# Query projections of head groups 2 to 8 by one level of Strassen's algorithm

## The chip, the cores and the metric

The kernel runs on one core of one Trainium2 chip. The metric is the device time of one execution in microseconds (us): before the change the median of 3 runs is 1006.12 us (1002.88 to 1007.81).

## The reference, cut to what matters

The program is one decoder layer in float32 on 8 blocks of 128 tokens with 512 channels: a Mamba2 mixer, a gated MLP, a cross attention with 32 query heads in 8 groups (each group has one key and value head), and a small gated LoRA layer, with norms between. The change touches the cross attention alone:

```python
for g in range(8):                              # head groups
    K = rms(ctx @ Wk[g].T) * k_norm_w           # 1024 x 128
    V = ctx @ Wv[g].T                           # 1024 x 128
    for h in range(4):                          # heads of the group
        Q = rms(x @ Wq[g, h].T) * q_norm_w      # x is 1024 x 512, Wq[g, h] is 128 x 512
        for b in range(8):                      # blocks of 128 tokens
            P = softmax(Q[b] @ K[b].T / sqrt(128) + mask)
            out[b] += (P @ V[b]) @ Wo[:, g, h].T
```

For a group, all of Q is one product: the weights (512 outputs by 512 channels) times the activations (512 channels by 1024 tokens).

## The kernel before, in words

Every engine has its own in-order instruction queue, written out by hand; engines meet through semaphores (`wait_ge`). A float32 operand is split into a rounded part and a remainder (`_hi`, `_lo`), and each product is three matmuls (`mm3`, L374 to L378): ScalarE writes `_hi`, GpSimd or VectorE subtracts it to give `_lo`.

The attention is a loop over groups g of eight slots jj, one for each block of 128 tokens. Slot jj does the attention of block jj, and beside it a piece of the projections that later slots need: n = jj // 4 is a half of the tokens, j = jj % 4. In each slot TensorE's queue (`slot` in the tensor block) holds, in this order:

- the query product of one head over 512 tokens (`q_step`, 12 matmuls of 512 columns, in banks 0 and 1), and the key and value products of one token block (`kv_step`, 12 matmuls of 256 columns, bank 2). Slots 3 and 7 have no `kv_step`; they begin with `kt_step` (L641), which transposes the normed keys in bank 0 or 1. Slots 0 and 4 have two `kv_step`
- `s_step` (L654), the scores of the next block in bank 3
- `pt_step` (L664), the transposes of this block's probabilities
- `d_step`, 12 matmuls: the output projection of the block before
- in slots 2 and 6 `qs_step` (L635), which folds the sums of squares of four heads in bank 7
- `pv_step`, 3 matmuls: probabilities times values.

The other queues follow it. VectorE in a slot: sum of squares of one head (`q_part`, L1864 and L1866), in slots 2 and 6 `k_var`, `softmax_max` (L1901, L1905), `pt_rest`, `v_rest`, in slots 2 and 6 `k_norm` (L1855), `add_out` (L1923), `softmax_rec` (L1910), in slots 2 and 6 `q_var` (L1877, reads bank 7), `ot_rest`. ScalarE: `q_evac` (L1129 squares a head, L1132 copies it), `kv_evac`, `pt_evac`, `softmax_exp` (L1161), rounding of weights (`wq_hi` L1106, `wkv_hi` L1097, `wo_hi` L1115), `ot_evac`. GpSimd: powers for the norms (`k_rsqrt`, `q_rsqrt`), `p_scale` (L1509: scales the probabilities of the next block), and the `_lo` parts of weights (L1327): four pieces of 512 columns of query weights, four of output weights in slot 0, two of key and value weights in slot 2. SyncE loads the weights of the next group when the buffers `raw_a` and `raw_b` come free.

`kt_step` in slot 3 belongs to the keys whose norm was made in slot 2; it waits only for that norm and for the bank:

```python
def kt_step(g, n):
    pe.wait_ge(kn_done, 2 * g + n + 1)
    wait_bank(g, 5 * n + 4)
```

The query heads of group g are spread: the four of tokens 512 to 1023 in slots 7 (of group g - 1), 0, 1 and 2, the four of tokens 0 to 511 in slots 3 to 6 of group g - 1. The last group therefore still has one head in each of slots 0, 1 and 2. The loop is `Fori(0, 7)` over groups, with slot 0 of group 0 before it and slots 1 to 7 of the last group behind it.

Of the kernel before, what the change touches and what calls it, by code (L numbers as in the profile page):

```python
# [29 lines left out]
def build_program(nc, x, ctx_t, mask, consts, fold_in, chan, rows, w_dt, w_in, w_out, w_gu, w_dn,  # L30
# [9 lines left out]
    with ctx:  # L40
# [11 lines left out]
        act_hi = sb(ctx, "act_hi", [P, KT, B * L], f32r)  # L52
        act_lo = sb(ctx, "act_lo", [P, KT, B * L], f32r)
        res = sb(ctx, "res", [P, B, DM])
        w_hi = sb(ctx, "w_hi", [P, 5120], f32r)
        w_lo = sb(ctx, "w_lo", [P, 5120], f32r)
        raw_a = sb(ctx, "raw_a", [P, 2048])
        raw_b = sb(ctx, "raw_b", [P, 2048])
        cst = sb(ctx, "cst", [P, 3 * P])
        ident, tri, strict = cst[:, 0:P], cst[:, P:2 * P], cst[:, 2 * P:3 * P]  # L60
        chan_sb = sb(ctx, "chan_sb", [P, NCONV * DCONV + NCONV + 2])
        qk_w = sb(ctx, "qk_w", [P, 1])
        pow_m = sb(ctx, "pow_m", [P, 16])
        xn = sb(ctx, "xn", [P, 2, DM])
# [9 lines left out]
        with ExitStack() as m:  # L74
            row_sb = sb(m, "row_sb", [P, 2 * DM + 3 * NH])
# [30 lines left out]
        with ExitStack() as m:  # L106
# [21 lines left out]
            ra_sb = sb(m, "ra_sb", [P, KT, NE + NE * RANK])  # L128
            bl_sb = sb(m, "bl_sb", [NE * RANK, DM])
            cmp_m = sb(m, "cmp_m", [P, 2, NE, NE])  # L130
            lg = sb(m, "lg", [P, B, NE])
            dif = sb(m, "dif", [P, B, NE, NE])
            beat = sb(m, "beat", [P, B, NE, 2, NE])
# [5 lines left out]
            midt = sb(m, "midt", [NE * RANK, B, P])  # L139
# [3 lines left out]
            with ExitStack() as early:  # L143
                q2 = sb(early, "q2", [P, 2, NTOK])
                q2t = sb(early, "q2t", [P, NTOK])
            x2t = sb(m, "x2t", [P, 2, KT, P])
            mid = sb(m, "mid", [P, B, NE, RANK])
# [64 lines left out]
        d_mm, d_add = sem("d_mm"), sem("d_add")  # L212

# [3 lines left out]
        dl_cp, dl_pool, a_sum, a_mean, a_ssq = (sem("dl_cp"), sem("dl_pool"), sem("a_sum"), sem("a_mean"),  # L217
                                                sem("a_ssq"))
# [11 lines left out]
        WQ_SLOT = {1: (0, 1), 3: (2,), 4: (3,)}  # L230
# [26 lines left out]

        def mamba_raw(p):

            return raw_b[:, (p - 4) * 512:(p - 3) * 512] if 4 <= p < 8 else raw_a[:, p % 8 * 512:(p % 8 + 1) * 512]  # L260
# [3 lines left out]
        def _(sp_eng):  # L264
# [18 lines left out]
            sp_eng.dma_start(cst[:, P:], consts[:, P:]).then_inc(ld_small[6], 16)  # L283
# [61 lines left out]
            sp_eng.dma_start(mask_sb[:, :], mask).then_inc(ld_small[4], 16)  # L345
            sp_eng.dma_start(ra_sb[:, :, :], w_ra).then_inc(ld_lora[0], 16)
            sp_eng.dma_start(bl_sb[:, :], w_b).then_inc(ld_lora[1], 16)

            def next_group(g):


                sp_eng.wait_ge(wq_l, 4 * g + 4)
                sp_eng.dma_start(raw_a[:, :], w_q[bass.ds(g + 1, 1)].rearrange("a p n -> (a p) n"))\
                    .then_inc(ld_q, 16)
                sp_eng.wait_ge(wo_l, 4 * g + 4)
                sp_eng.dma_start(raw_b[:, 0:1024], w_kv[bass.ds(g + 1, 1)].rearrange("a p n -> (a p) n"))\
                    .then_inc(ld_kv, 16)
                sp_eng.wait_ge(wkv_l, 2 * g + 4)
                sp_eng.dma_start(raw_b[:, :], w_o[bass.ds(g + 1, 1)].rearrange("a p n -> (a p) n"))\
                    .then_inc(ld_o, 16)  # L360

            with sp_eng.Fori(0, GROUPS - 1) as g:
                next_group(g)
# [7 lines left out]
        def _(pe):  # L371
# [232 lines left out]
            def q_step(g, n, h):  # L604

                pe.wait_ge(wq_l, 4 * g + h + 1)
                r = 5 * n + h
                wait_bank(g, r)
                tok = slice(n * NTOK, (n + 1) * NTOK)
                for k in range(KT):  # L610
                    c0 = WQ_COL[h] + k * P
                    t = mm3(bank[r % 2][:, :], w_hi[:, c0:c0 + P], w_lo[:, c0:c0 + P],
                            act_hi[:, k, tok], act_lo[:, k, tok], k == 0, k == KT - 1)
                t.then_inc(q_mm, 1)

            def wait_bank(g, r):


                pr = (r - 2) % 10
                gg = g if r >= 2 else g - 1  # L620
                if isinstance(gg, int) and gg < 0:
                    return
                n, hh = pr // 5, pr % 5
                if hh < 4:
                    pe.wait_ge(q_ev, 8 * gg + 4 * n + hh + 1)
                else:
                    pe.wait_ge(kt_ev, 2 * gg + n + 1)

            def qs_step(g, n):
# [3 lines left out]
                if not (isinstance(g, int) and u == 0):  # L633
                    pe.wait_ge(qv_done, u)
                mm(bank[7][:, 0:GH * 16], fold[:, :], qpart[:, n, :], start=True, stop=True).then_inc(qs_mm, 1)  # L635

            def kt_step(g, n):
                pe.wait_ge(kn_done, 2 * g + n + 1)
                wait_bank(g, 5 * n + 4)
                for j in range(HALF):  # L640
                    t = nc.tensor.transpose(bank[(5 * n + 4) % 2][:, j * P:(j + 1) * P], kraw[:, j, :], ident)  # L641
# [48 lines left out]
            def slot(g, jj, lead=True, before=True):  # L690

                n, j = jj // HALF, jj % HALF
                pg, pn = (g, 1) if n == 0 else (g + 1, 0)
                if j == 0:
                    kv_step(pg, pn, 0)
                if j < 3:
                    q_step(pg, pn, j + 1)
                    kv_step(pg, pn, j + 1)
                else:
                    kt_step(pg, pn)  # L700
                    if lead:
# [1476 lines left out]
```

## Time and profile before

| | us |
|---|---|
| three runs | 1002.88, 1006.12, 1007.81 (median 1006.12) |
| the profiled execution, its own time | 1007.58 |
| its span in the profile | 1005.8 |
| TensorE busy in the span | 966.1 (96%) |
| VectorE, ScalarE, GpSimd busy | 573.8, 494.2, 404.0 |
| mean granted TensorE clock | 0.986 of full |

The profile page gives busy times by engine and by line; the timeline gives each instruction with its start and duration, and in brackets how long its engine sat idle before it and who released it. The duration of a matmul in it is longer than its share of the engine, because matmuls overlap: what one costs is the distance from one start to the next. A windows row is the busy time of each engine in a stretch, with the granted clock.

### The profile page before, as it was taken

To read this page: it belongs to the slowest core of one execution; us is meant where nothing else is said; L and a number is where in the kernel's file an instruction comes from. 1 tells how busy PE (TensorE), PEld (TensorE's weight loads), DVE (VectorE), ACT (ScalarE), POOL (GpSimd) and SP (SyncE) were. 2 spreads that over 40 slices of the span, in tenths; PEclk is the share of its full clock that TensorE was granted. 3 is DMA by queue.
4 is the path that set the end of the run, shared out by engine and by line. 5 is a ranking of instruction groups with operands and counts; after the bars stand their busy time and mean duration, and the time that the engine had idled before them with its cause. 6 is when DMAs were issued, how large, how long until landed. Compare 5 with 4: busy or idle time off the path is not lost.

```text
span 1005.8 us, 15353 instructions
## 1 busy us (share of the span) xinstructions
PE 966.1 (96%) x5010; PEld 804.8 (80%) x5010; DVE 573.8 (57%) x1340; ACT 494.2 (49%) x1368; POOL 404.0 (40%) x341
## 2 busy tenths in 40 slices
PE   5999799999999999899999999999999999999895
PEld 3866488878888888788888888888888888888782
DVE  3665554422321357566666666666566666666777
ACT  4655342422231246555654654654655555555554
POOL 4334634744443453342442442532622623514322
PEclk9999999999999999899999999999999999999997
DMA  6200013310111111011010020020020020100002
GB/s 218 82 3 31 12 46 125 105 63 0 63 63 63 44 62 56 22 43 43 22 54 29 21 83 0 21 83 0 21 83 0 27 78 0 63 0 0 1 1 85
DMA packets 12977, 45.60 MB, mean 45 GB/s; under 512 B 1617, under 2 KB 2257, under 8 KB 9873
## 3 DMA queue, kind: packets, MB, share of 16 engines
q1 hardware_dynamic: 12944, 45.20, 12.9%
q8 instruction: 17, 0.28, 0.1%
q14 instruction: 16, 0.12, 0.0%
HBM read 43.10 MB, written 2.10 MB: 45 GB/s over the span
## 4 chain that ended last, share of the span: by engine, by line
PE 86%; DVE 5%; POOL 3%; ACT 2%; issue 2%; DMA 1%; SPq 0%; POOLq 0%; DVEq 0%; ACTq 0%
PE bank L376 25%; PE bank L378 24%; PE bank L377 24%; PE bank L654 6%; PE bank L664 3%; PE bank L387 1%; POOL res L1438 1%; DVE cbuf L1638 1%; POOL rstd L1333 1%; PE bank L641 1%; DVE bst L1775 1%; POOL h_lo L1327 1%; DMA res<-in_x 1%; PE bank L455 1%; PE bank L744 0%
## 5 line engine op out<-in xcount | busy, mean ns | idle before, releaser
L376 PE MATMUL bank<-act_hi,w_hi 128*128 128x512 f32 x560 | 225.0, 402 | 2.0 <-DVE act_lo L1585 1.6
L378 PE MATMUL bank<-act_hi,w_lo 128*128 128x512 f32 x560 | 220.0, 393 | 0.0
L377 PE MATMUL bank<-act_lo,w_hi 128*128 128x512 f32 x560 | 220.0, 393 | 0.0
L1509 POOL TENSOR_TENSOR pb<-pb,prec 128x512 f32<-128x512 f32 x64 | 66.6, 1040 | 311.6 <-DVE prec L1910 311.6
L1161 ACT ACTIVATE pb<-pb,nmax 128x128 f32<-128x128 f32 x256 | 99.8, 391 | 79.1 <-DVE nmax L1905 79.1
L376 PEld LDWEIGHTS bank<-act_hi,w_hi 128*128 128x128 f32 x560 | 106.1, 189 | 25.6 <-issue 4.3
L378 PEld LDWEIGHTS bank<-act_hi,w_lo 128*128 128x128 f32 x560 | 106.1, 189 | 22.9
L377 PEld LDWEIGHTS bank<-act_lo,w_hi 128*128 128x128 f32 x560 | 106.2, 190 | 22.7 <-issue 1.4
L376 PE MATMUL bank<-w_hi,ot_hi 128*128 128x512 f32 x256 | 105.0, 410 | 0.8 <-DVE ot_lo L1585 0.8
L378 PE MATMUL bank<-w_hi,ot_lo 128*128 128x512 f32 x256 | 100.9, 394 | 0.0
L377 PE MATMUL bank<-w_lo,ot_hi 128*128 128x512 f32 x256 | 100.3, 392 | 0.0
L1327 POOL TENSOR_TENSOR w_lo<-raw_b,w_hi 128x512 fp32r<-128x512 f32 x70 | 89.2, 1298 | 10.4 <-ACT w_hi L845 10.4
L1129 ACT ACTIVATE q<-bank 128x512 f32<-128x512 f32 x64 | 38.2, 597 | 106.9 <-PE bank L378 106.9
L1327 POOL TENSOR_TENSOR w_lo<-raw_a,w_hi 128x512 fp32r<-128x512 f32 x66 | 85.0, 1306 | 4.2 <-ACT w_hi L845 2.2
L1327 POOL TENSOR_TENSOR h_lo<-hb,h_hi 128x512 fp32r<-128x512 f32 x28 | 37.4, 1336 | 120.5 <-ACT h_hi L1052 120.5
L1809 DVE TENSOR_TENSOR hb<-sg,bank 128x512 f32<-128x512 f32 x28 | 19.2, 687 | 115.9 <-ACT sg L1044 115.9
L1864 DVE STREAM_TRANSPOSE q2t<-q 128x512 f32<-128x512 f32 x64 | 45.3, 708 | 68.6 <-ACT q L1129 68.4
L1044 ACT ACTIVATE sg<-bank 128x512 f32<-128x512 f32 x28 | 16.7, 598 | 130.0 <-PE bank L378 130.0
L1901 DVE SCALAR_TENSOR_TENSOR pb<-bank,qr,mask_sb 128x128 f32<-128x128 f32 x256 | 71.9, 344 | 12.4 <-PE bank L654 11.1
L376 PE MATMUL bank<-w_hi,ctx_hi 128*128 128x256 f32 x256 | 72.3, 282 | 2.0 <-DVE kraw L1800 2.0
L1585 DVE TENSOR_TENSOR pt_lo<-bank,pt_hi 128x512 fp32r<-128x512 f32 x64 | 43.7, 683 | 51.1 <-ACT pt_hi L1169 51.1
L378 PE MATMUL bank<-w_hi,ctx_lo 128*128 128x256 f32 x256 | 72.0, 281 | 0.0
(190 smaller groups left out, 2066.4 us busy)
## 6 DMA issues: line engine op xcount, KB each, us to landing
raw_a<-in_w_q SPq DMA_DIRECT2D x8, 1024.0 KB, 4.8
raw_b<-in_w_o SPq DMA_DIRECT2D x8, 1024.0 KB, 4.8
raw_a<-in_w_gu SPq DMA_DIRECT2D x7, 1024.0 KB, 5.3
raw_b<-in_w_kv SPq DMA_DIRECT2D x8, 512.0 KB, 3.3
raw_b<-in_w_dn SPq DMA_DIRECT2D x7, 512.0 KB, 3.3
res<-in_x SPq DMA_DIRECT2D x8, 256.0 KB, 6.1
raw_b<-in_ctx_t SPq DMA_DIRECT2D x8, 256.0 KB, 3.2
xre<-in_x SPq DMA_DIRECT2D x2, 1024.0 KB, 7.0
```

Source lines behind the costliest of these rows:

```text
L376: mm(o, l_hi, r_hi, start=first, stop=False)
L377: mm(o, l_hi, r_lo, start=False, stop=False)
L378: return mm(o, l_lo, r_hi, start=False, stop=last)
L654: t = mm(bank[3][:, h * L:(h + 1) * L], q_t[:, n, h, tok], k_t[:, n, tok], start=True, stop=True)
L664: t = nc.tensor.transpose(bank[4][:, h * L:(h + 1) * L], pb[:, jj % 2, h, :], ident)
L1129: A(q2[:, h % 2, :], bank[(5 * n + h) % 2][:, :], ACT.Square).then_inc(qsq_done, 1)
L1161: t = A(pb[:, jj % 2, h, :], pb[:, jj % 2, h, :], ACT.Exp, bias=nmax[:, jj % 2, h:h + 1], accum_out=psum_[:, jj % 2, h:h + 1])
L1327: TT(dst, src, f32(hi), ALU.subtract).then_inc(done, 1)
L1509: TT(pb[:, jj % 2, :, :], pb[:, jj % 2, :, :], prec[:, jj % 2, :].unsqueeze(2).to_broadcast([P, GH, L]), ALU.mult).then_inc(p_norm, 1)
L1585: TT(dst, src, f32(hi), ALU.subtract).then_inc(done, 1)
L1864: V.transpose(q2t[:, :], q2[:, h % 2, :]).then_inc(qtr_done, 1)
L1901: t = STT(pb[:, jj % 2, h, :], bank[3][:, h * L:(h + 1) * L], qr[:, 4 * n + h, j:j + 1], mask_sb[:, :], ALU.mult, ALU.add)
```

## The change

Of the product weights times activations the weights are cut in four blocks (two by two heads, two by two halves of the channels: A11, A12, A21, A22 with 256 x 256 numbers each) and the activations in four (B11, B12, B21, B22: half of the channels by half of the tokens). Before, each head and token half took four channel steps: eight block products. Now, for groups 2 to 8, seven block products P1 to P7 of sums of blocks give the same four results (Strassen's algorithm in Winograd's form). One product is 2 (heads) x 2 (channel steps) x 3 = 12 matmuls of 512 columns. Group 1 (g = 0) is computed as before, its last three heads together in slot 0.

- The sums of activation blocks T1 to T4 are made once, in group 0: 20 operations of 512 columns on GpSimd (`combine_t3` and `combine_t1`, 12 of them, in slot 0; `combine_t2`, 6, in slot 1; `combine_t4`, 2, in slot 3), each waiting for the one before it, all ahead of `p_scale` of their slot. ScalarE rounds them, VectorE makes the remainders (`t_round`, `t_rest`).
- The sums of weight blocks are made per group, 4 operations on GpSimd (`combine_s`, `combine_s1`, `combine_s4`), and each of the seven operands is rounded and split on its own: 7 pieces on ScalarE and GpSimd for 4 (`wp_hi`, `wp_rest`).
- The sums of products are made by VectorE (`q_add`, 12 operations of 512 columns per group that read a bank), ScalarE (`q_copy`, 2) and GpSimd (`combine_u4`, 4).
- Product i of group g + 1 stands in slot i + 1 of group g; slot 0 has no product, and the last group's slots have none.
- `kt_step` uses bank 7 in place of bank 0 or 1 and so waits for `q_var` as well.
- The squares come from the copied heads in place of the banks (`q_square`), in another order of heads.
- Buffers of the Mamba part and of the last layer share their place with others; w_q is loaded in four blocks. Groups 0 and 6 are written out, the loop runs over 1 to 5 (VectorE and TensorE: 1 to 6).

The diff, cut to its core (in order: SyncE's loads, TensorE's product, `kt_step` and slot, ScalarE's `wp_hi` and slot, GpSimd's `combine_s`, `t_op` and slot, VectorE's slot):

```diff
+        WP_COL = [1024, 1536]
+        A11, A12, A21, A22 = 0, 1, 2, 3
+        BLOCK_AT = [A11, A11, A12, A21, A11, A12, A22]
+        PART_EARLY = {5: (1, 0, 3), 6: (1, 0, 1), 0: (0, 1, 0), 1: (0, 1, 1), 2: (0, 1, 3)}
+        PART_LATE = {4: (1, 0, 2), 5: (1, 0, 0), 1: (0, 1, 2)}
+        def prod_at(gn, i):
+            return 14 * gn - 6 + 2 * i
+        def split_at(gn, i):
+            return 7 * gn - 3 + i
...
+            def next_group(g, more=True):
+                sp_eng.wait_ge(wo_l, 4 * g + 1)
+                if not first_group(g):
+                    load_quad(A21, g + 1, ld_a2)
+                    sp_eng.wait_ge(wq_l, split_at(g, 6) + 1)
+                    load_quad(A22, g + 1, ld_a2)
...
+            def q_prod(gn, i):
+                pe.wait_ge(wq_l, split_at(gn, i) + 1)
+                if isinstance(gn, int) and gn == 1 and i in (1, 2, 3, 6):
+                    pe.wait_ge(t_lo, {2: 2, 1: 4, 3: 6, 6: 8}[i])
...
             def kt_step(g, n):
                 pe.wait_ge(kn_done, 2 * g + n + 1)
-                wait_bank(g, 5 * n + 4)
+                if first_group(g) and n == 0:
+                    pe.wait_ge(q_ev, 3)
+                else:
+                    pe.wait_ge(qv_done, 2 * g + n + 1)
...
+            def slot(g, jj, make=True, before=True):
                 n, j = jj // HALF, jj % HALF
                 pg, pn = (g, 1) if n == 0 else (g + 1, 0)
+                behind = first_group(g) and jj in (2, 3)
                 if j == 0:
                     kv_step(pg, pn, 0)
-                if j < 3:
-                    q_step(pg, pn, j + 1)
+                if not before:
+                    q_step(1, 1)
+                if j == 3:
+                    kt_step(pg, pn)
+                if jj == 2:
                     kv_step(pg, pn, j + 1)
-                else:
-                    kt_step(pg, pn)
-                    if lead:
-                        q_step(g + 1, n, 0)
+                if make and jj and not behind:
+                    q_prod(g + 1, jj - 1)
+                if j < 3 and jj != 2:
+                    kv_step(pg, pn, j + 1)
+                if not before:
+                    q_step(1, 2)
+                    q_step(1, 3)
                 s_step(*((g, jj + 1) if j < 3 else (pg, 4 * pn)))
                 pt_step(g, jj)
...
                 pv_step(g, jj)
+                if make and behind:
+                    q_prod(g + 1, jj - 1)
...
+            def wp_hi(gn, i):
+                act.wait_ge(*((ld_q, 16 * gn + 16) if i == 0 else (ld_a12, 16 * gn) if i == 5 else
+                              (ld_a2, 32 * gn) if i == 6 else (s_cmb, 8 * gn - 8 + (0, 2, 1, 3, 4)[i])))
+                act.wait_ge(q_mm, prod_at(gn, i - 2) + 2 if i >= 2 else prod_at(gn, 0) - 2 * i)
...
+                if make and jj < 7 and jj != 1:
+                    wp_hi(g + 1, jj)
                 pt_evac(g, jj)
                 softmax_exp(*((g, jj + 1) if j < 3 else (pg, 4 * pn)))
+                if make and jj == 1:
+                    wp_hi(g + 1, jj)
...
+            def combine_s(gn):
+                pool.wait_ge(ld_a2, 32 * gn)
+                pool.wait_ge(*((wq_l, 4) if isinstance(gn, int) and gn == 1 else (wo_l, 4 * gn - 2)))
+                TT(quad(A12), quad(A11), quad(A21), ALU.subtract).then_inc(s_cmb, 1)
+                pool.wait_ge(s_cmb, 8 * gn - 7)
+                pool.wait_ge(wq_l, split_at(gn, 0) + 1)
+                TT(quad(A11), quad(A22), quad(A12), ALU.subtract).then_inc(s_cmb, 1)
...
+            def t_op(o, x, y, op):
+                if t_count[0]:
+                    pool.wait_ge(t_step, t_count[0])
+                TT(o, x, y, op).then_inc(t_step, 1)
+                t_count[0] += 1
...
                 if j == 2:
                     k_rsqrt(pg, pn)
+                if make and jj == 1:
+                    combine_s(g + 1)
+                    wp_rest(g + 1, 1)
+                    combine_s1(g + 1)
+                if make and jj == 4:
+                    combine_s4(g + 1)
+                if make and jj < 7 and jj != 1:
+                    wp_rest(g + 1, jj)
+                if make and jj == 4:
+                    combine_u4(g + 1)
+                if first_group(g):
+                    if jj == 0:
+                        pool.wait_ge(q_mm, 4)
+                        pool.wait_ge(n_lo, 24)
+                        combine_t3()
+                        combine_t1()
+                    elif jj == 1:
+                        combine_t2()
+                    elif jj == 3:
+                        combine_t4()
                 p_scale(*((g, jj + 1) if j < 3 else (pg, 4 * pn)))
...
+                if make and jj in (3, 4, 5, 7) and not (start and jj == 3):
+                    q_add(g + 1, jj - 1)
                 if j < 3:
-                    q_part(pg, pn, j + 1)
-                    if j == 2:
-                        k_var(pg, pn)
                     softmax_max(*turn)
                     pt_rest(g, jj)
+                    if make and (jj == 6 or jj == 2 and not start):
+                        q_add(g + 1, jj - 1)
                     v_rest(pg, pn, j + 1)
                     if j == 2:
                         k_norm(pg, pn)
```

## Rows read from the trace of the kernel before

**Rows 1.** The page's busy line of TensorE, and the windows of one of the loop's groups

```profile
PE 966.1 (96%) x5010; PEld 804.8 (80%) x5010; DVE 573.8 (57%) x1340; ACT 494.2 (49%) x1368; POOL 404.0 (40%) x341
...
600.50:673.40 72.90, 72.90 (x423) 63.81 (x422) 47.56 (x117) 41.23 (x133) 28.57 (x22) 1.00 0.11 36
```

**Rows 2.** Timeline of TensorE, slots 1 to 3 of one group (start, us, what)

```profile
636.26 1.05 PE L654 MATMUL bank<-k_t,q_t 128*128 128x128 f32 x8
...
641.04 0.39 PE L376 MATMUL bank<-act_hi,w_hi 128*128 128x512 f32 x1
...
643.77 0.28 PE L376 MATMUL bank<-w_hi,ctx_hi 128*128 128x256 f32 x1
...
645.18 1.05 PE L654 MATMUL bank<-k_t,q_t 128*128 128x128 f32 x8
646.07 0.60 PE L664 MATMUL bank<-cst,pb 128*128 128x128 f32 x4
646.43 0.47 PE L376 MATMUL bank<-w_hi,ot_hi 128*128 128x512 f32 x1
...
649.41 0.48 PE L376 MATMUL bank<-pt_hi,v_hi 128*128 128x512 f32 x1
...
650.19 0.60 PE L641 MATMUL bank<-cst,kraw 128*128 128x128 f32 x4
```

**Rows 3.** Timeline of VectorE in slot 2 of the same group

```profile
646.28 1.12 DVE L1901 SCALAR_TENSOR_TENSOR pb<-bank,qr,mask_sb 128x128 f32<-128x128 f32 x4 [0.17 <-PE bank L654]
647.43 0.69 DVE L1905 TENSOR_REDUCE nmax<-pb 128x4 f32<-128x512 f32 x1
648.04 0.68 DVE L1585 TENSOR_TENSOR pt_lo<-bank,pt_hi 128x512 fp32r<-128x512 f32 x1
...
649.22 0.69 DVE L1855 TENSOR_TENSOR kraw<-kraw,kv 128x512 f32<-128x512 f32 x1
649.83 0.68 DVE L1923 TENSOR_TENSOR res<-res,bank 128x512 f32<-128x512 f32 x1
650.43 0.17 DVE L1910 RECIPROCAL prec<-psum_ 128x4 f32<-128x4 f32 x1
650.52 0.69 DVE L1877 TENSOR_SCALAR qv<-bank 32x16 f32<-32x16 f32 x4
```

**Rows 4.** Timelines of ScalarE (slot 2) and GpSimd (slots 0 and 1), same group

```profile
649.71 1.14 ACT L1097 ACTIVATE w_hi<-raw_b 128x512 fp32r<-128x512 f32 x2
...
633.46 5.03 POOL L1327 TENSOR_TENSOR w_lo<-raw_b,w_hi 128x512 fp32r<-128x512 f32 x4
641.39 1.04 POOL L1509 TENSOR_TENSOR pb<-pb,prec 128x512 f32<-128x512 f32 x1 [2.90 <-DVE prec L1910]
```

**Rows 5.** A GpSimd sum of two SBUF tensors (ns min/median/max), and loads of 256 KB

```profile
L1438 POOL TENSOR_TENSOR res<-res,xre x8: 1281/1298/1748, 186.6 to 200.1; 128x512 f32<-128x512 f32 x8
...
raw_b<-in_ctx_t SPq DMA_DIRECT2D x8, 256.0 KB, 3.2
```

**Rows 6.** Timeline of TensorE: its idle times in group 0 and at the end

```profile
404.58 0.36 PE L376 MATMUL bank<-w_hi,ctx_hi 128*128 128x256 f32 x1 [1.98 <-DVE kraw L1800]
...
411.23 0.50 PE L376 MATMUL bank<-pt_hi,v_hi 128*128 128x512 f32 x1 [2.10 <-DVE pt_lo L1585]
...
950.77 0.66 PE L664 MATMUL bank<-cst,pb 128*128 128x128 f32 x4 [1.57 <-POOL pb L1509]
```

**Rows 7.** Windows behind these idle times (PEclk is third from the end)

```profile
404.95:409.00 4.05, 4.05 (x23) 3.93 (x22) 2.54 (x7) 0.53 (x3) 2.26 (x2) 0.58 0.00 0
...
412.00:415.10 3.10, 3.10 (x8) 2.35 (x8) 0.87 (x2) 0.85 (x3) 1.04 (x1) 0.50 0.00 0
...
951.00:954.40 3.40, 3.12 (x16) 2.37 (x14) 3.37 (x9) 1.10 (x4) 0.47 (x1) 1.00 0.00 0
```

**Rows 8.** Window of one slot of the last group, from scores to scores

```profile
927.45:936.40 8.95, 8.95 (x54) 7.84 (x53) 6.69 (x17) 4.47 (x15) 3.84 (x4) 1.00 0.00 1
```

More of the change, by code:

```diff
@@ L346, in _ @@
+            sp_eng.wait_ge(wq_l, 4)
+            load_quad(A11, 1, ld_q)
+            load_quad(A21, 1, ld_a2)
+            load_quad(A22, 1, ld_a2)
+            next_group(0)
+            with sp_eng.Fori(1, GROUPS - 2) as g:
+                next_group(g)
+            next_group(GROUPS - 2, more=False)
+            sp_eng.wait_ge(q_mm, prod_at(GROUPS, 0))
             sp_eng.dma_start(ra_sb[:, :, :], w_ra).then_inc(ld_lora[0], 16)
             sp_eng.dma_start(bl_sb[:, :], w_b).then_inc(ld_lora[1], 16)
[L349 to L360, printed above, removed]
@@ L362, in _ @@
-            with sp_eng.Fori(0, GROUPS - 1) as g:
-                next_group(g)
             for b in FIN:
@@ L726, in _, with group @@
             s_step(0, 0)
-            slot(0, 0, before=False)
-            with pe.Fori(0, GROUPS - 1) as g:
+            def group(g):
                 for jj in range(1, 8):
@@ L731, in _ @@
                 slot(g + 1, 0)
+            slot(0, 0, before=False)
+            group(0)
+            with pe.Fori(1, GROUPS - 1) as g:
+                group(g)
             def lora_in(b):
@@ L1224, in _, with group @@
             softmax_exp(0, 0)
-            slot(0, 0)
-            with act.Fori(0, GROUPS - 1) as g:
+            def group(g, more=True):
                 for jj in range(1, 8):
                     slot(g, jj)
-                slot(g + 1, 0, refill=False)
+                slot(g + 1, 0, make=more)
+            slot(0, 0)
+            group(0)
+            with act.Fori(1, GROUPS - 2) as g:
+                group(g)
+            group(GROUPS - 2, more=False)
             def x2_evac(b):
@@ L1541, in _, with group @@
             wo_rest(0, 3)
-            slot(0, 0)
-            with pool.Fori(0, GROUPS - 1) as g:
+            def group(g, more=True):
                 for jj in range(1, 8):
                     slot(g, jj)
-                slot(g + 1, 0, refill=False)
+                slot(g + 1, 0, make=more)
+            slot(0, 0)
+            group(0)
+            with pool.Fori(1, GROUPS - 2) as g:
+                group(g)
+            group(GROUPS - 2, more=False)
             last = GROUPS - 1
             for jj in range(1, 4):
-                slot(last, jj, refill=False)
+                slot(last, jj, make=False)
                 rsqrt(23 + jj)
@@ L1972, in _, with group @@
             softmax_max(0, 0)
-            slot(0, 0, before=False)
-            with dve.Fori(0, GROUPS - 1) as g:
+            def group(g):
                 for jj in range(1, 8):
@@ L1977, in _ @@
                 slot(g + 1, 0)
+            slot(0, 0, before=False)
+            group(0)
+            with dve.Fori(1, GROUPS - 1) as g:
+                group(g)
             def ln2(i):
@@ L2080, in _ @@
             for jj in range(1, 4):
-                slot(last, jj, lead=False)
+                slot(last, jj, make=False)
                 b = jj - 1
```

396 lines of the change are left out of this document (289 added, 107 removed).

## The prediction

> **What bounds the kernel now.** I read the page's busy line first: TensorE 96% of the span, no other engine over 57% [rows 1]. The average hides stages, so the windows of the attention loop came next: in all six groups that I cut, TensorE is busy for the whole 72.8 us at full clock, VectorE 47.5, ScalarE 41.2, GpSimd 28.6 [rows 1]. So inside the loop a matmul removed is worth its full distance, as long as nothing makes TensorE wait; and any wait that the change adds is lost time in full, for there is no idle time to take it up. The third view, the timeline of TensorE beside those of the others, tells how near the waits are. In slot 2 the transposes of the keys start at 650.19 right behind the last matmul [rows 2], and their input, the normed keys, was ready at about 649.8 (VectorE issues its next operation then) [rows 3]. The next thing on VectorE's queue that matters here, the read of bank 7 (L1877), ends only at 650.52 + 0.69 = 651.21 [rows 3].
>
> **The saving.** One head costs 643.77 - 641.04 = 2.73 us [rows 2], 0.228 us per matmul of 512 columns (the 0.39 us shown overlap). Before, a group has eight of these pieces, after it has seven products of 12 matmuls each. Seven groups change: 7 x 2.73 = **-19.1 us**.
>
> **The key transposes in slots 3 and 7.** They now write bank 7 and wait for `q_var`, which stands in the slot before, behind the softmax, the key norm, `add_out` and the reciprocal. Even with VectorE's queue as it is, 651.21 is 1.0 us later than 650.19. And in slots 2 and 6 the change puts two sums of products (`q_add`) ahead of all this. Such a sum reads one bank and one SBUF tensor like L1923, whose start is 0.60 us ahead of its successor's [rows 3]: 1.2 us more. VectorE's row of work starts with the scores of the same slot and runs without a gap, so nothing catches up. TensorE waits 1.0 + 1.2 + 0.1 for the signal = 2.3 us. What stands behind the transposes waits too: product, scores, everything of the slot. This happens in slot 7 of groups 0 to 6 and in slot 3 of groups 1 to 6 (in slot 3 of group 0 a product stands in front and covers it): 13 x 2.3 = **+29.9 us**. From below, if the sums fit into gaps, 1.0 each (13); from above, with `q_add` at two of its distances, 3.5 each (46).
>
> **The second product, slot 2.** Its weights are the last of a chain that passes four engines. GpSimd ends the output weights of slot 0 at 638.49, which is 2.2 us behind the scores of slot 1 (636.26) [rows 2, 4]. Then come the two sums of `combine_s`, 1.3 us each [rows 5]; until 4.9. ScalarE is through with its exponentials at about scores + 4.5 (649.71 against 645.18) [rows 2, 4], so the rounding (0.6, half of L1097's 1.14 [rows 4]) starts at 5.0, and the remainder (1.3) ends, with signals, at 7.0. TensorE is at that product at scores + 4.8 (641.04 - 636.26) + 1.4 for the keys = 6.2 [rows 2]. Six groups wait 0.8: **+4.8 us** (0 to 12). The loads of A21 and A22 are issued when the first output weight is split (about 634.8) and take some 3.2 us [rows 5], so they are in time. This work delays `p_scale` of slot 1 by some 3.5 us, to scores + 9.5; it is wanted at about 6.2 + 0.8 + 2.7 + 0.9 = 10.6: covered, by 1 us. In slot 4 four more GpSimd sums stand ahead of `p_scale`; they leave about 1 us as well. The seven weight pieces instead of four, and the other `q_add`, lie beside 70 us of TensorE on engines that are busy for 29 to 48 us [rows 1] and come a slot ahead: nothing.
>
> **Group 0.** Here GpSimd makes the activation sums, in the queue ahead of `p_scale`. From the end of the last query head in slot 0: copy of the head and rounding of the first block on ScalarE 1.4 us, its remainder 1.3, twelve sums at 1.3 each [rows 5] 15.6, the scale 1.04 [rows 4]: 19.4 us. TensorE has in that time scores 0.9, transposes 0.4, the wait for `pt_lo` that it has today (2.1 [rows 6]), values 0.8, product 2.7, keys 1.4, scores 0.9: 9.1. It waits **10.3 us** in slot 1. Then, until the scale of slot 2: `combine_s` 2.6, the weight piece 1.6, `combine_s1` 1.3, six sums 7.8, scale 1.0 = 14.3, against 0.4 + 2.8 + 0.8 + 1.4 + 0.9 = 6.3 us of TensorE: **8.0 us**. The product P2 behind slot 2 wants T2 rounded and split behind the exponentials and the key weights: 7.1 against 4.1: **3.0 us**. Together **+21.3 us**. With 1.04 us per sum, the nearest cheaper GpSimd row [rows 4], it is some 15; with the 1.75 that the slowest row of L1438 shows [rows 5], 29.
>
> **The last group.** Its slots lose their query heads, and they are no longer bound by TensorE. A slot there is 8.95 us with VectorE busy for 6.7 [rows 8]; without the head TensorE would need 6.2, while slot 1 gets a second `q_part` (1.35) on VectorE. I take 8.1 and 7.0 for two slots in place of 6.2, and 1.0 at the transposes of slot 3: **+3.7 us** (1 to 7).
>
> **The clock.** TensorE's idle times of 1.98 and 2.10 us [rows 6] were each followed by a stretch at the lower level, 1.2 GHz for 2.4 (PEclk 0.58 and 0.50 [rows 7]); the one of 1.57 us was not (1.00) [rows 6, 7]. One stretch has 3.4 us at half clock and costs some 1.6. A bubble of 2.3 us lies above both that had this effect, but near them, so between none (0) and all 13 (21 us) I take half: +10.4, and one more in group 0, where most of the slow time lies inside the next wait: **+12.0 us**. The Trainium skill (TensorE: Matmul & The Clock Gate, HAM oscillation) names longer gaps than 2.3 us as the ones to avoid. By that rule the loop's bubbles would not slow the clock, and the sum would be 10.4 us less; rows 6 and 7 speak against it, since both gaps there were shorter.
>
> **The sum.** -19.1 + 29.9 + 4.8 + 21.3 + 3.7 + 12.0 = +52.6 us. The profiled execution took 1007.58 us (span 1005.8 and 1.8 around it), 1.5 above the median of 1006.12. So 1060 us for it and 1059 for the median.
>
> **The rivals.**
> - *The clock stays up at the loop's bubbles.* For it: the 1.57 us gap had no effect [rows 7]. Against: both at 2 us had. It gives 1059 - 10 = 1049 us. This is what the skill's page would have, too.
> - *The clock falls at all 13.* For it: two of two gaps of 2 us. Then 6.5 more stretches x 1.6 = +10: 1069 us.
> - *The activation sums hide.* GpSimd's twelve sums in slot 0 are one long row of single operations; if they ran at half the time or the scale did not stand behind them, group 0 would cost a few us: 1059 - 18 = 1041 us. Against it: each waits for the one before.
> - *The other side: the transposes don't wait.* One mechanism: the read of bank 7 comes before TensorE gets to slots 3 and 7, as VectorE's queue would be ahead of TensorE's by then. Its price is the 29.9 us and the clock behind them (10.4): 1059 - 40 = 1019. It decides from the point where the waits left sum to less than the 19.1 us saved, so it must take most of the GpSimd row of group 0 with it (one cause: queues that run ahead by a slot): 1006 - 19 = 987 us. For it: VectorE is busy only 47.5 of 72.9 us [rows 1]. Against it: its row of work in slot 2 begins with scores that TensorE has just made, and it stands in order [rows 3].
>
> **How the numbers follow.** Half of the clock falls, the forecast: 0.45. Clock stays: 0.2. Clock always falls: 0.14. Sums hidden: 0.1. The other side at or near 987: 0.05. The rest (0.06) is mixed cases, half of them near no change. A change under 0.5% can't be told from none with this kernel; so faster 0.05, same 0.03, slower 0.92. The range runs from below the case of the hidden sums, 1030, to above that of the clock with a VectorE row longer by 1 us at each transpose, 1085.
>
> **What would show it.** In the changed profile, the key transposes (L641 before) have idle time of about 2.3 us ahead of each of 13, released by VectorE's `q_var`; a group of the loop takes 72.9 - 2.7 + 4.6 + 0.8 = 75.6 us, or 77 with slow stretches; the transposes of probabilities in slots 1 and 2 of group 0 wait 10 and 8 us for GpSimd. 84 matmuls of 512 columns are gone. If the transposes' idle time is below 1 us, my step on bank 7 is wrong; if groups are 70 us long, the whole of it.

## The result, and the profile after

The changed kernel takes **1118.0 us** (median of 4 runs, 1113.5 to 1122.6) beside 1006.8 us of the kernel before on the same chip: ratio 1.112, 95% interval 1.108 to 1.115. The forecast was 1059 us, range 1030 to 1085. Slower is right, and the loss is twice the size: 111 us for 53. The profiled execution took 1113.8 us, its span 1112.0, that is 106.2 more than before.

The page's busy and clock lines of the changed kernel (for [rows 1]):

```profile
PE 984.6 (89%) x4926; PEld 812.9 (73%) x4926; DVE 637.5 (57%) x1432; ACT 489.5 (44%) x1355; POOL 528.8 (48%) x438
...
PEclk9999999999999997998998998999998998998897
```

The 84 matmuls are gone (5010 to 4926), and TensorE is nevertheless busy for 18.5 us more and idle for 87.7 us more. The windows of two groups of the loop, with the columns of [rows 1], show that it is the same in each:

```profile
586.16:671.49 85.33, 76.35 (x413) 65.84 (x414) 55.70 (x129) 39.87 (x129) 43.17 (x35) 0.94 0.10 31
671.49:756.80 85.31, 76.47 (x413) 65.89 (x413) 55.18 (x129) 40.37 (x130) 43.20 (x34) 0.94 0.10 31
```

A group takes 85.3 us where it took 72.9, with TensorE idle for 9.0. The timeline of TensorE has four places for it in each group (start, duration, what, idle before and releaser):

```profile
586.16 0.63 PE L763 MATMUL bank<-cst,kraw 128*128 128x128 f32 x4 [2.20 <-DVE qv L2178]
...
600.34 0.41 PE L470 MATMUL bank<-w_hi,ctx_hi 128*128 128x256 f32 x1 [3.02 <-DVE kraw L2079]
...
620.28 0.49 PE L470 MATMUL bank<-t,w_hi 128*128 128x512 f32 x1 [1.56 <-POOL w_lo L1502]
...
630.54 0.63 PE L763 MATMUL bank<-cst,kraw 128*128 128x128 f32 x4 [2.19 <-DVE qv L2178]
```

In order: key transposes of slot 7, the second key and value product of slot 0, the product of slot 2, key transposes of slot 3. The waits view sums them over the span (us in total, times, longest):

```profile
PE bank L763 <- DVE qv L2178: 30.1, 14, 2.2
PE bank L470 <- DVE kraw L2079: 24.2, 8, 3.0
PE bank L786 <- POOL pb L1765: 19.7, 3, 10.2
...
PE bank L470 <- POOL w_lo L1502: 9.2, 8, 1.7
PE bank L470 <- DVE pt_lo L1864: 7.1, 3, 3.1
```

The second of these lines is the one that the forecast does not have at all. The first is its 2.3 us at 13 places (2.2 us measured) and one wait more, of 1.6 us, in the last group. VectorE's row in slot 2 (for [rows 3]) is as it was added up:

```profile
624.26 1.13 DVE L2202 SCALAR_TENSOR_TENSOR pb<-bank,qr,mask_sb 128x128 f32<-128x128 f32 x4 [1.30 <-PE bank L776]
...
626.63 1.28 DVE L2161 TENSOR_TENSOR q_t<-w_raw,bank 128x512 f32<-128x512 f32 x2
627.82 0.28 DVE L1864 TENSOR_TENSOR v_lo<-bank,v_hi 128x128 fp32r<-128x128 f32 x1
...
629.70 0.69 DVE L2178 TENSOR_SCALAR qv<-bank 32x16 f32<-32x16 f32 x4
```

The two sums take 627.82 - 626.63 = 1.19 us, and the read of bank 7 ends at 630.4, where TensorE starts.

**The account.** Terms of the forecast beside the trace, in us of the span:

| term | forecast | trace |
|---|---|---|
| 84 matmuls less | -19.1 | -19.1 |
| key transposes, slots 3 and 7 | +29.9 (13 x 2.3) | +30.1 (14 waits) |
| second key product, slot 0 | none | +22.2 (24.2, 2.0 of it there before) |
| weights of the second product | +4.8 | +9.2 |
| group 0 | +21.3 | +21.3 (10.2 + 8.4 + 2.7), and 5.0 more at its values and the last group's |
| last group | +3.7 | in the lines above |
| TensorE slower | +12.0 | +37.6 (18.5 + 19.1) |
| sum | +52.6 | +106.3 (the span's rise: 106.2) |

The last term is what TensorE's busy time rose by, without the matmuls that are gone. The mean clock fell from 0.986 to 0.953. One stretch of 3.4 us at half clock costs 1.7, so that clock and span give (1 - 0.953) x 1112 / 1.7 = 31 stretches, for 8 to 9 before: 22 to 23 more, 37 to 39 us. By place the granted clock shows 10 more behind key transposes, 8 more at slot 0 of groups 1 to 7 (one fall there is of double length), 3 more in group 0, and 2 more ahead of the last key transposes; outside the attention it is one less ahead and one more behind.

### The profile page after: what moved, and what is told of

Its sections match the earlier page's. It is cut to its first block, busy times and chain, and to the rows that moved or that the text cites. A ratio compares the mean times of both kernels' runs of the same rounds, so it can differ in the third digit from the quotient of the medians.

```text
span 1112.0 us, 15673 instructions
## 1 busy us (share of the span) xinstructions
PE 984.6 (89%) x4926; PEld 812.9 (73%) x4926; DVE 637.5 (57%) x1432; ACT 489.5 (44%) x1355; POOL 528.8 (48%) x438
## 4 chain that ended last, share of the span: by engine, by line
PE 58%; DVE 14%; issue 10%; POOL 9%; ACT 5%; DMA 2%; SPq 0%; DVEq 0%; POOLq 0%; ACTq 0%
PE bank L470 17%; PE bank L471 16%; PE bank L472 16%; PE bank L776 4%; POOL w_lo L1502 3%; DVE pb L2202 3%; ACT pb L1313 2%; DVE q_t L2161 2%; DMA raw_a<-in_w_q 1%; PE bank L786 1%; POOL t_raw L1694 1%; DVE nmax L2206 1%; PE bank L763 1%; DVE q2t L2143 1%; POOL res L1613 1%
## 5 line engine op out<-in xcount | busy, mean ns | idle before, releaser
L470 PE MATMUL bank<-act_hi,w_hi 128*128 128x512 f32 x448 | 179.0, 400 | 1.7 <-DVE act_lo L1864 1.6
L471 PE MATMUL bank<-act_lo,w_hi 128*128 128x512 f32 x448 | 175.2, 391 | 0.0
L472 PE MATMUL bank<-act_hi,w_lo 128*128 128x512 f32 x448 | 175.2, 391 | 0.0
L1502 POOL TENSOR_TENSOR w_lo<-raw_a,w_hi 128x512 fp32r<-128x512 f32 x101 | 130.3, 1302 | 85.8 <-ACT w_hi L1246 81.5
L470 PEld LDWEIGHTS bank<-act_hi,w_hi 128*128 128x128 f32 x448 | 84.5, 189 | 21.2 <-issue 3.9
L471 PEld LDWEIGHTS bank<-act_lo,w_hi 128*128 128x128 f32 x448 | 84.6, 189 | 18.5 <-issue 1.4
L472 PEld LDWEIGHTS bank<-act_hi,w_lo 128*128 128x128 f32 x448 | 84.4, 188 | 18.1
L470 PE MATMUL bank<-w_hi,ctx_hi 128*128 128x256 f32 x256 | 75.6, 295 | 24.2 <-DVE kraw L2079 24.2
L1321 ACT ACTIVATE pt_hi<-bank 128x512 fp32r<-128x512 f32 x64 | 38.3, 599 | 112.5 <-PE bank L786 112.5
L471 PE MATMUL bank<-w_lo,ctx_hi 128*128 128x256 f32 x256 | 74.5, 291 | 0.0
L776 PE MATMUL bank<-k_t,q_t 128*128 128x128 f32 x512 | 72.7, 288 | 1.6 <-issue 1.6
```

Of the source, the lines that this page charges most:

```text
L470: mm(o, l_hi, r_hi, start=first, stop=False)
L471: mm(o, l_hi, r_lo, start=False, stop=False)
L472: return mm(o, l_lo, r_hi, start=False, stop=last)
L776: t = mm(bank[3][:, h * L:(h + 1) * L], q_t[:, n, h, tok], k_t[:, n, tok], start=True, stop=True)
L1321: A(pt_hi[:, :], bank[4][:, :], ACT.Copy).then_inc(pthi_done, 1)
L1502: TT(dst, src, f32(hi), ALU.subtract).then_inc(done, 1)
```

## The experiments

Each was timed beside the kernel before (1005.7 to 1007.2 us). "Changed" is 1118 us. Times are medians of four executions, and the profiled one can differ from them (1113.8 for 1118.0 us in the changed kernel), so idle and busy times are compared between profiled executions.

### The missing term: slot 0

Bank 2 takes both key and value products of slot 0. Before, a head's product stood between them. The first experiment gives the second one bank 0, with the waits that this needs: for the last read of bank 0 ahead of it, and for its own read-out ahead of the next product:

```diff
+            if n == 1 and j == 1 and not (isinstance(g, int) and g == 0):
+                return bank[0]
             return bank[2 + j % 2] if isinstance(g, int) and g == n == 0 else bank[2]
...
+                elif n == 1 and j == 1 and not first_group(g):
+                    pe.wait_ge(q_ev, 8 * g + 8)
...
+                    pe.wait_ge(kraw_done, 8 * gn - 2)
```

> The changed kernel, with the second key and value product of slot 0 written to bank 0 in place of bank 2, so that it need not wait until the first one is read out. Theory (each bubble of TensorE is lost in full, and the half-clock stretch behind it too): 7 groups lose their 3.0 us wait in slot 0, 21 us, and up to 7 slow stretches of 1.7 us with it; 1085 to 1097 us for 1118. Rival (the sum of the added work on VectorE and GpSimd sets the pace): the wait comes back a slot later, less than 8 us gained.

Measured: **1083.1 us**, ratio 1.077 (1.075 to 1.078), 35 less, 2 us below the expected range. The 3.0 us waits of groups 1 to 7 are gone, the other three stay at 2.19, 1.78 and 2.18. Between the profiled executions, 31.6 us apart, 21 us are idle time and 11 are time in which TensorE is busy, and five to six half-clock stretches went (26 left of 31). So one missing line of the account is worth a third of the loss.

### The key transposes: three ways

`read_first` moves VectorE's read of bank 7 directly behind the key norm, ahead of the two sums, `add_out` and the reciprocal:

```diff
+                        q_var(pg, pn)
                     if make and (jj == 6 or jj == 2 and not start):
                         q_add(g + 1, jj - 1)
...
-                if j == 2:
-                    q_var(pg, pn)
```

> The changed kernel, with the read of bank 7 right behind the key norm in VectorE's queue, ahead of the product sums, the residual add and the reciprocal; nothing else. Theory of bubbles: the wait of the key transposes falls from 2.2 to about 0.3 us, 13 times, 25 us, and up to 22 us of slow stretches with it; 1070 to 1093. Rival: the reciprocal now comes 0.6 us later and the wait moves to the transposes of the probabilities; under 8 us gained.

Measured: **1082.7 us**, ratio 1.076 (1.075 to 1.078), as the theory has it. The waits fell to 0.34 us, the stretches from 31 to 24 or 25.

`behind` instead moves the products of slots 2 and 6 behind the values, so that they are TensorE's work while VectorE reads (and their sums to the end of VectorE's slot):

```diff
-                behind = first_group(g) and jj in (2, 3)
+                behind = jj in (2, 6) or first_group(g) and jj == 3
```

> The changed kernel, with products 2 and 6 of slots 2 and 6 behind the values in TensorE's queue, and their sums at the end of VectorE's slot, as group 0 has it in slot 2. The product then covers the wait of the key transposes for bank 7, and comes later than its weights. Theory of bubbles: 13 waits of 2.2 us and 6 of 1.5 go, 37 us, and up to two slow stretches per group (22 us) with them; 1058 to 1081 us. Rival (work of the engines): under 12 us gained.

Measured: **1096.7 us**, ratio 1.091 (1.086 to 1.096), 16 above the expected range and 21 less than the changed kernel. In the loop the transposes no longer wait, but TensorE's timeline has new places:

```profile
581.98 0.50 PE L470 MATMUL bank<-pt_hi,v_hi 128*128 128x512 f32 x1 [1.03 <-DVE pt_lo L1864]
...
619.00 0.66 PE L786 MATMUL bank<-cst,pb 128*128 128x128 f32 x4 [3.22 <-POOL pb L1765]
```

With the product away from its old place, scores and the transposes of the probabilities made from them are 2.7 us of TensorE closer, and the softmax of that block (VectorE, ScalarE, GpSimd in turn) is no longer covered. A piece of TensorE's work hides two chains, the one behind it and the one in front of it; moving it takes cover from one to give it to the other.

`between` puts the product between transposes and output projection of slots 2 and 6, `p_scale` of slot 1 ahead of the weight remainder on GpSimd, and on VectorE the sums behind the key norm and the read of bank 7 ahead of `add_out`:

```diff
                 pt_step(g, jj)
+                if make and between:
+                    q_prod(g + 1, jj - 1)
```

> The changed kernel, with products 2 and 6 between the transposes of probabilities and the output projection of slots 2 and 6, the scale of slot 1 ahead of the second weight piece on GpSimd, and in slots 2 and 6 VectorE's key norm ahead of the product sums and its read of bank 7 ahead of the residual add. The product then stands between the scores and the key transposes, and still between the scores and the next transposes of probabilities. Theory: the waits of 2.2 and 1.6 us go without a new one in the place of the 3.2 us that the kernel named behind got; 1052 to 1072. Rival: a new wait of some 3 us per group for GpSimd's scale, 1085 to 1097.

Measured: **1080.4 us**, ratio 1.075 (1.071 to 1.078), 8 above the range, and without the new wait of the rival. The waits of a group are 0.70 (transposes of slot 7), 3.03 (slot 0), 0.38 (product) and 1.38 (transposes of slot 3). So the key transposes kept 13.7 us of their 30.1 where I had counted on none. In slot 2 of group 0 waits of 8.4 and 2.7 us turned into 2.2, 2.9 and 6.1, with nothing gained. Slot 0's wait, left in place, still took the clock down in 6 of 7 groups.

### Do the two repairs add?

`keys_read` is the first two experiments together.

> Both earlier edits together: the second keys of slot 0 in bank 0, and VectorE's read of bank 7 ahead of the product sums. Each alone gained 35 us. Theory (bubbles add up, because TensorE has no slack of its own): 70 us less than the changed kernel, 1043 to 1053. Rival (they share a cause, such as one clock stretch counted twice, or the pace of VectorE): less than 55 us gained, 1063 or more.

Measured: **1053.8 us**, ratio 1.047 (1.044 to 1.051), 64 less, 0.8 us above the range; the parts alone gave 35 and 35. They add but for 6 us, with 21 stretches left; the rival (under 55 us) falls.

### The wait and the clock, measured in the kernel before

The kernel before has no Strassen products and its loop has no idle time, so it can price one bubble. `before_wait` adds the wait for `q_var` to the key transposes and nothing else:

```diff
                 wait_bank(g, 5 * n + 4)
+                if not (isinstance(g, int) and g == n == 0):
+                    pe.wait_ge(qv_done, 2 * g + n + 1)
```

> The kernel before with the one wait alone: the key transposes also wait for VectorE's read of bank 7, as it stands there. 15 bubbles of 1.0 to 1.1 us. If the clock only falls behind the longer bubbles (2.0 us and more did it, 1.6 us did not), it costs 16 us and no more: 1022 to 1024. If short bubbles cost clock as well, 1035 or more.

Measured: **1022.2 us**, ratio 1.017 (1.016 to 1.019), 16.5 more. `before_wait2` adds to it two VectorE sums of 512 columns behind the key norm, into a buffer that nothing reads:

```diff
                         k_norm(pg, pn)
+                        for m in range(2):
+                            TT(xn[:, m, :], q2t[:, :], q2t[:, :], ALU.add)
```

> The kernel before, with one wait and two operations more: the key transposes also wait for the read of bank 7, and two sums of 512 columns stand behind the key norm in VectorE's slots 2 and 6, which gives 15 bubbles of 2.2 us and nothing else: 33 us. If the clock falls at none, 1039 us; at half of them, as I forecast, 1052; at all, 1064. This measures the forecast's terms on the key transposes and on the clock by themselves.

Measured: **1057.2 us**, ratio 1.052 (1.048 to 1.056), 50 more. The waits view of TensorE, of the first and then of the second:

```profile
PE bank L643 <- DVE qv L1879: 15.0, 15, 1.0
```

```profile
PE bank L643 <- DVE qv L1879: 33.0, 15, 2.2
```

18 us more of waits, 35 us more of time. The rest is the clock: behind the fifteen waits of 1.0 us it never fell (mean 0.990); behind those of 2.2 us it fell eleven times of fifteen, first in a steady turn of two with and one without (behind the fifteenth another wait of 0.8 us followed at once). Two windows of the second kernel, each right behind such a wait (columns of [rows 7]):

```profile
589.31:593.31 4.00, 4.00 (x15) 3.20 (x14) 0.37 (x1) 0.69 (x1) 4.00 (x3) 0.64 0.00 0
629.72:633.72 4.00, 4.00 (x25) 3.49 (x24) 0.38 (x1) 1.45 (x3) 3.03 (x2) 1.00 0.00 0
```

The total is 17.4 stretches for 8.6, so nearly nine more in the balance (two of group 0 and one of the first 130 us went away). This is the forecast's own step on the key transposes, measured alone: between the profiled executions 33.0 + 8.8 x 1.7 = 48.0 of 48.2 us (50 between the medians). So the wait of the key transposes was sized rightly and its clock somewhat low: "half of them" was 11 of 15 here and 10 of 13 in the changed kernel. That the clock term as a whole was three times too small has more causes, counted below.

### Group 0

`t_on_vector` moves the 20 activation sums from GpSimd to VectorE's queue (`pool.wait_ge` to `dve.wait_ge`, the same calls behind the first read-out of the keys in slot 0 and near the end of slots 1 and 3).

> The changed kernel, with the twenty sums of activation blocks on VectorE in place of GpSimd (twelve in slot 0 of group 0 behind the first read-out of keys, six at the end of slot 1, two at the end of slot 3). Theory of bubbles: the waits of 10.2, 8.4 and 2.7 us in slots 1 and 2 of group 0 fall to about 3 together, 18 us, with some 3 to 6 us of half clock; 1093 to 1098. Rival (the clock and the bubbles further on set the end; GpSimd had been late for its weight pieces too): under 8 us gained.

Measured: **1111.1 us**, ratio 1.103 (1.101 to 1.105), only 7 less, 13 above the range and inside the rival's (under 8). The wait of 10.2 us fell to 2.0 and that of 8.4 is gone, but others came, as VectorE is the engine that also makes `q_part`; TensorE's timeline:

```profile
440.43 0.69 PE L754 MATMUL bank<-qpart,fold 128*128 128x64 f32 x2 [4.11 <-DVE qpart L2090]
...
448.46 0.77 PE L470 MATMUL bank<-t,w_hi 128*128 128x512 f32 x1 [3.97 <-issue]
```

Idle time from group 0's start to slot 0 of the next fell by 9.0 us (35.9 to 26.9), and 35 half-clock stretches in place of 31 gave the larger part back.

`short_sums` leaves the sums on GpSimd and cuts them to 16 columns; T1 to T4 are then an activation block as it is. This prices the sums alone:

```diff
-                TT(o, x, y, op).then_inc(t_step, 1)
+                TT(o[:, 0:16], x[:, 0:16], y[:, 0:16], op).then_inc(t_step, 1)
```

> The changed kernel with the 20 activation sums of group 0 cut from 512 to 16 columns; T1 to T4 are then taken from an activation block as it is, so the first group of products computes other numbers, with every wait and every other instruction in place. It prices the sums in place, on GpSimd. Theory (group 0 costs what the GpSimd row costs, 10.2 and 8.4 us of waits less what was there before): both waits fall under 2 us, 14 to 18 us less, 1100 to 1104 us of 1118. Rival (the clock takes part of it back, as it did when the sums were put on VectorE): 1104 to 1112 us. Against both, below 1097 us, would be that the sums held up more than slots 1 and 2.

Measured: **1100.4 us**, ratio 1.092 (1.089 to 1.094), 17.6 less: at the lower end of the range, so the forecast's group 0 is right in size and in cause. Between the profiled executions TensorE is idle for 16.0 us less and busy for 5.6 us more, so in that pair the clock did take a part back; the medians don't show it. A wait of 4.0 us in slot 1 stays in place of 10.2, above the 2 us expected; the one of 8.4 is gone altogether.

### All repairs together

`keys_between_t` is `keys_bank0`, `between` and `t_on_vector`.

> The edits of keys_bank0, between and t_on_vector together. If all bubbles of the loop are gone, a group takes 70.1 to 71 us for 72.85 in the kernel before, and what stays is some 12 us in group 0, 5 in the last group, and their clock: 1000 to 1022 us. If VectorE or GpSimd has become the bound in any slot, a group takes over 73 and the kernel over 1030.

Measured: **1038.3 us**, ratio 1.032 (1.028 to 1.036): above the range, at the rival's numbers. A group takes 73.4 us, with TensorE waiting 0.7 and 1.4 us in it for VectorE's read of bank 7. `tuned` mends what its trace showed as next: in slot 1 ScalarE's `ot_evac` goes ahead of the weights' rounding, VectorE reads bank 7 ahead of the sums and makes the squares of the heads from slot 7 on, and of group 0's sums those of slot 1 stand behind the last `q_part`, with the remainders of T3 behind those of T2 in slot 2:

```diff
                 if make and jj == 1:
+                    ot_evac(g, jj)
                     wp_hi(g + 1, jj)
...
+            return {5: (1, 0, 3), 6: (1, 0, 1), 7: (1, 1, 0), 0: (0, 1, 1), 1: (0, 1, 2)}.get(jj)
```

> keys_between_t with what its trace shows to be late put right: in slot 1 ScalarE's read-out of the values ahead of the second weight piece; sums of squares of the four later heads from slot 7 on, so that VectorE has none at the head of slot 2; VectorE's read of bank 7 ahead of the product sums; in group 0 the squares ahead of the sums of T2. Theory: a group falls from 73.4 to 70.5 to 71.5 us, below the 72.85 of before, and the kernel to 1015 to 1028 us; group 0 and the last group keep it above the kernel before. Rival: moved work reappears as a wait elsewhere in the group, over 72.85 us and over 1032.

Measured: **1031.2 us**, ratio 1.025 (1.023 to 1.027), between the two cases (1015 to 1028, over 1032). The windows of two groups, columns as above:

```profile
571.60:644.25 72.65, 71.60 (x409) 61.29 (x409) 55.56 (x129) 39.64 (x130) 42.64 (x33) 1.00 0.12 36
644.25:716.43 72.18, 71.51 (x408) 61.25 (x409) 55.55 (x129) 39.67 (x130) 42.66 (x33) 1.00 0.11 36
```

At last a group is shorter than before (72.4 for 72.9) and at full clock, but 12 matmuls less should have given 70.2, and idle time explains only 0.7 to 1.0 of the difference. Part of the rest hides in what counts as busy: TensorE's timeline behind a wait of 0.24 us

```profile
643.60 0.40 PE L485 MATMUL bank<-pt_hi,v_lo 128*128 128x512 f32 x1
644.25 0.63 PE L779 MATMUL bank<-cst,kraw 128*128 128x128 f32 x4 [0.24 <-DVE qv L2191]
644.87 0.50 PE L483 MATMUL bank<-t_hi,w_hi 128*128 128x512 f32 x1
```

has 0.62 us from the start of the four transposes to the next matmul. Before it was 0.35:

```profile
649.96 0.39 PE L378 MATMUL bank<-pt_hi,v_lo 128*128 128x512 f32 x1
650.19 0.60 PE L641 MATMUL bank<-cst,kraw 128*128 128x128 f32 x4
650.54 0.48 PE L376 MATMUL bank<-act_hi,w_hi 128*128 128x512 f32 x1
```

Here 644.87 - 643.60 = 1.27 us pass from the last value matmul to the first of the product, for 0.58 before: 0.45 us more than the 0.24 shown. The two key transposes of a group thus lose 0.9 of the 2.2 us; some 0.4 us stay unexplained.

`tuned_short` is this version with the sums cut to 16 columns, to ask whether the method would pay with the sums for nothing.

> The same cut of the 20 activation sums (to 16 columns, other numbers in T1 to T4) in the most mended version, where the sums stand on VectorE. Theory: what is left of the cost (1031 against 1006 us) is group 0 with its clock and the last group, since the loop's groups take 72.4 us against 72.9; the sums are about half of group 0, so 1014 to 1020 us, still above the kernel before. Rival: the sums are nearly all that is left and the time comes below 1008 us, so that the method would pay with the sums made elsewhere.

Measured: **1026.2 us**, ratio 1.019 (1.018 to 1.021), 5 less and 6 above the range. It would not. The sums were not what group 0 waits for any more; the product behind slot 2 waits 8.0 us (7.3 in `tuned`), and starts 0.1 us behind a row of four remainders on VectorE:

```profile
445.07 0.77 PE L483 MATMUL bank<-t,w_hi 128*128 128x512 f32 x1 [8.00 <-issue]
```

```profile
440.35 4.62 DVE L1833 TENSOR_TENSOR t<-act_hi,t 128x512 fp32r<-128x512 f32 x4
```

The first is TensorE's timeline and the second VectorE's. The row holds the remainders of T2 and then T3, and this product reads T2 alone. Two kept traces show what the row costs. In `keys_between_t` T2's remainders stood here by themselves (two in 1.28 us, done at 448.76), and in `tuned` T3's had been moved behind them (four in 4.62 us, done at 450.83). The product starts 0.1 us behind the row in both:

```profile
448.86 0.76 PE L472 MATMUL bank<-t,w_hi 128*128 128x512 f32 x1 [3.96 <-issue]
```

```profile
450.94 0.77 PE L483 MATMUL bank<-t,w_hi 128*128 128x512 f32 x1 [7.30 <-issue]
```

So `tuned` repaired slot 1 and lengthened this wait by some 3 us by its own order (its semaphore counts both pairs). No run has T3's remainders elsewhere with the rest of `tuned` in place. No version here beats the kernel before.

## Why the prediction was wrong, and where it was right

- **"The saving": the step that failed.** It took 2.73 us for each of the eight heads' pieces replaced by seven, in full, and so also the one of slot 0 that has no successor. That piece stood between two products that use bank 2 in turn, and covered the way of the keys through ScalarE, VectorE's `ot_rest`, and the copy that frees the bank. In the changed kernel a `q_part` stands on that way too. Slot 0, from the last matmul of the first product to TensorE's start at 600.34:

```profile
597.04 0.28 PE L472 MATMUL bank<-w_hi,ctx_lo 128*128 128x256 f32 x1
...
597.77 0.69 DVE L1864 TENSOR_TENSOR ot_lo<-bank,ot_hi 128x512 fp32r<-128x512 f32 x1 [0.30 <-ACT ot_hi L1327]
598.38 0.70 DVE L2143 STREAM_TRANSPOSE q2t<-q 128x512 f32<-128x512 f32 x1
599.11 0.69 DVE L2145 TENSOR_REDUCE qpart<-q2t 128x16 f32<-128x512 f32 x1
...
599.91 0.28 DVE L2079 COPY kraw<-bank 128x128 f32<-128x128 f32 x1
```

  The same places in slot 0 of the kernel before, where the second product starts at 625.92 without a wait:

```profile
623.03 0.28 PE L378 MATMUL bank<-w_hi,ctx_lo 128*128 128x256 f32 x1
...
624.57 0.28 DVE L1800 COPY kraw<-bank 128x128 f32<-128x128 f32 x1
...
625.92 0.28 PE L376 MATMUL bank<-w_hi,ctx_hi 128*128 128x256 f32 x1
```

  So removing 2.73 us of work opened 3.02 us of idle time, a loss. The copy starts 1.5 us behind the last matmul before and 2.9 us behind it now. By these rows (an estimate, no run separates the two) 1.3 of the 3.0 us come from the squares that the change put ahead of the copy, which the forecast's account does not have either, and 1.7 from the missing cover. The clue stood in [rows 6]: TensorE's 1.98 us wait in group 0 is for the same copy, there even with a query head between the two products, and I used it for the clock alone. `keys_bank0` shows the size: 35 us with its clock.
- **"The clock": a count that was too low in every place.** 23 stretches more, not 7: +37.6 for +12.0. Half of the 13 bubbles of 2.3 us, the forecast said; 10 of 13 it was (3.5 stretches too few), and 11 of 15 in `before_wait2`. At slot 0, where the forecast had no bubble, the clock fell in all seven groups from 1 on (8 stretches). Group 0 had 3 more where one was forecast, and the last group 2 where none was. Of the 54 us between the forecast's sum and the span's rise, 22 are slot 0's idle time and 26 the clock.
- **The rule of the Trainium skill.** The rows went against it: gaps of 2.2 us were followed by stretches at 1.2 GHz in eleven of fifteen cases. TensorE: Matmul & The Clock Gate of the Trainium skill (HAM oscillation) names longer gaps than these as the ones to avoid. Here the measurement decides, and the forecast was right to go by [rows 6, 7].
- **"The second product": 1.56 us, not 0.8.** The step called the loads of A21 and A22 in time. In the chain of the changed kernel the load is the longest link ahead of that product:

```profile
611.82 3.32 DMA raw_a<-in_w_q
...
615.30 1.30 POOL raw_a L1657
...
616.77 1.28 POOL raw_a L1660
...
618.88 1.28 POOL w_lo L1502
```

  It is issued when the first output weight is split (610.9 here), and the two sums, the rounding and the remainder follow it to 620.2. I had GpSimd's own row end last. 3 us of load were right in length and wrong in their place.
- **Right:** the key transposes (13 of 2.2 us for 13 of 2.3, and 1.6 in the last group for 1.0), VectorE's row behind them, group 0 with 10.2, 8.4 and 2.7 for 10.3, 8.0 and 3.0, and the direction.
- **The rivals.** "Clock always falls" named the right sense and would have given 1069. "Sums hide" and "transposes don't wait" are refuted by the waits. None had a bubble that I hadn't listed: the range held sizes of known terms and no missing one.

## What to carry to other kernels

On an engine that is busy for the whole loop, a piece of work that is taken away must be asked two things: what it costs, and whose latency it hides. Follow every bank and buffer that is used on both sides of the gap it leaves, in every slot where it disappears. Look, too, at what is put ahead of the operation that frees it. Then price a new bubble with the clock that it may take: here a wait of 1.0 us cost 1.1, one of 2.2 us 3.4 (16.5 and 50 us for fifteen), and one of 3.0 us some 5 (35 us for the seven of `keys_bank0`).

## What the runs showed of the hardware

- **How the clock answers to the length of a wait.** No fall behind the waits of 1.0 us (0 of 15, `before_wait`), nor behind those of 1.3 to 1.7 (0 of 5, the product's in the changed kernel). The product's waits of 1.60 to 1.94 us had none of 5 in `keys_bank0`, but those of 1.85 to 1.92 had 3 of 4 in `keys_read`. Behind 2.2 us it fell in 11 of 15 (`before_wait2`), 10 of 13 (key transposes of the changed kernel), 8 of 13 (`t_on_vector`, `short_sums`) and 6 of 13 (`keys_bank0`). At the waits of 3.0 us in slot 0 of groups 1 to 7 it fell in 7 of 7 (changed kernel, `t_on_vector`, `short_sums`), 6 of 7 (`between`, `behind`) and 5 of 7 (`read_first`); the changed kernel's wait of 3.0 us in group 0 had none. So the falls get more frequent with the length, but waits of one length differ with the kernel around them, and what decides there isn't shown. At 1.98 us the kernel before had a fall and `before_wait`, at 1.99, none.
- **A wait costs more than its bracket.** From the start of the last value matmul to the first matmul behind the key transposes TensorE takes 650.54 - 649.96 = 0.58 us before (timeline above); with a bracket of 1.00 us (`before_wait`) 1.78, with 2.20 (`before_wait2`) 2.99, and with 0.34 us (`keys_read`) 1.37. That is 0.2 us more than shown for each long wait, and 0.45 for the short one.
- **VectorE and GpSimd slow each other.** The remainders of T2 and T3 are one form, and in `tuned` they took (ns, min/median/max):

```profile
L1832 DVE TENSOR_TENSOR t<-t_raw,t x4: 681/1215/1748, 446.2 to 449.1; 128x512 fp32r<-128x512 f32 x4
```

  GpSimd split the key and value weights beside them, two in 3.12 us, where one beside an operation on a bank took 1.27. A sum of two SBUF tensors is thus priced at 0.68 us alone and up to 1.75 beside such work of GpSimd. The Trainium skill (GPSIMD Engine Reference, Specifications) says that the two share their SBUF interfaces, and names VectorE instructions with two SBUF inputs among those that contend. These rows agree.
